# A recommender forward pass on one NeuronCore: one gram matmul a sample, grams and layer 4 moved inside other layers, and one store of rows

## The chip, the cores and the metric

The kernel runs on one core of a Trainium2 chip. The metric is the device time of one execution in microseconds, as the median over runs. In the text, TensorE (PE) multiplies matrices from SBUF into PSUM, VectorE (DVE) and ScalarE (ACT) work elementwise on SBUF and PSUM, GpSimd (POOL) here issues the gathers, and SyncE (SP) issues loads and stores. Each engine runs its own instructions in order; semaphores tie them together.

## What is computed

For each of 512 samples, 26 rows of 128 numbers are fetched from an embedding table, a small dense network adds a 27th, all pairs of the 27 are multiplied, and four dense layers and a last product follow.

```python
fm = emb_table[jnp.arange(N_CAT)[None, :], cat_idx]          # 512 x 26 x 128
h = jax.nn.relu(dense_x @ Wd1 + bd1)                         # 13 -> 512
h = jax.nn.relu(h @ Wd2 + bd2)                               # 512 -> 256
dense = jax.nn.relu(h @ Wdf + bdf)                           # 256 -> 128
Z = jnp.concatenate([fm, dense[:, None, :]], axis=1)         # 512 x 27 x 128
S = jnp.einsum('bie,bje->bij', Z, Z)                         # the gram of a sample, 27 x 27
iu, ju = np.triu_indices(N_CAT + 1, k=1)
x = jnp.concatenate([S[:, iu, ju], dense], axis=-1)          # 351 pairs and dense
x = jax.nn.relu(x @ Wt1 + bt1)                               # layer 1, 479 -> 1024
x = jax.nn.relu(x @ Wt2 + bt2)                               # layer 2, 1024 -> 1024
x = jax.nn.relu(x @ Wt3 + bt3)                               # layer 3, 1024 -> 512
x = jax.nn.relu(x @ Wt4 + bt4)                               # layer 4, 512 -> 256
return jax.nn.sigmoid(x @ Wo + bo)
```

All of it is float32. Layers 2 and 3 split weights and activations into a high and a low float32r part and add three products, (high, high), (low weights), (low activations), in place of one float32 product.

## The kernel before

The batch is cut into four tiles of 128 samples (t = 0 to 3). A start computes the dense network for all samples, and its share of layer 1 (pre), while weights are loaded, split by ScalarE (split_hi) and VectorE (split_lo), and the first rows are gathered. GpSimd issues 104 gathers, one for each tile and feature, into a ring of 38 row buffers (rows); from the 39th on each waits until TensorE has turned the group of features whose buffer it takes.

For every tile, the features come in seven groups g of up to four. TensorE turns a group (transpose_features, L343) into a bank of PSUM (gp), and ScalarE (even g) or VectorE (odd g) copies it into zt (features, L507 and L637), where four samples q stand side by side. Then come the grams (gram, L356): 32 matmuls a tile, each with four samples as 128 stationary columns and the same four as 4 x 27 moving columns. Of each result only the four 27 x 27 blocks on the diagonal are wanted. ScalarE and VectorE copy these out in four rounds (extract, L519 and L645) into s_ij, VectorE turns them in 32 x 32 squares (turn_sums, L653) into xb, both copy the 351 pairs into xp (L524, L655), TensorE turns them in three pieces (transpose_pairs, L369), and ScalarE copies the result to xt (L526). Layer 1 (L380) needs xt.

Layer 1 has 8 column blocks m of 3 matmuls; layer 2 (L409) 48 products in two halves; layer 3 (L429) 24 products n. A sum is added to its bias by VectorE (L659, L670, L681), turned by TensorE (turn, L389) and passed through a relu by ScalarE (L530, L534, L538); VectorE makes the low part (L664, L675). Layer 4 (L445) and the last product (last_layers, L686 and L688) follow, then a sigmoid (L542) and a store of 128 single numbers a tile (L275).

The order on each engine is written out by hand. FEATURES_1, FEATURES_2 and FEATURES_3 say ahead of which m or n of each layer the next tile's feature groups are turned. GRAM_FROM says from which product n of layer 3 on one gram of the next tile follows each product; the rest of the grams stand behind layer 3, with the turn of layer 3's sum after TURN_AFTER of them, then layer 4 and the pairs. Turn 1 of layer 2 (the second half) stands ahead of product 12 of layer 3, which is the first product that needs it:

```python
                    if n == PRODUCTS_3 // 2:
                        turn(t, 1)
                    k, part = n // 3, n % 3
                    if k % 4 == 0 and part == 0:
                        pe.wait_ge(a2_hi, 2 * t + k // 4 + 1)
```

In tile 0 the last copies of features, features(0, 5) on VectorE and features(0, 6) on ScalarE, stand behind the split of the first two pieces of w3.

## Time and profile before

| | |
|---|---|
| Median of 3 runs | 223.09 us (221.65 to 224.78) |
| Span of the profiled execution | 278.7 us |
| Mean granted TensorE clock in it | 0.852 of full speed |
| TensorE matmuls busy | 189.4 us (68%), 976 records |
| TensorE weight loads busy | 148.4 us (53%), 976 records |
| VectorE busy | 82.0 us (29%), 123 |
| ScalarE busy | 66.0 us (24%), 114 |
| GpSimd busy | 104.4 us (37%), 111 |

The profiled execution is some 56 us longer than the timed ones. Busy times are shares of its span. TensorE's matmul time overlaps its weight loads (PEld), and ends of matmuls are modelled.
### The profile page before, as it was taken

To read this page: it belongs to the slowest core of one execution; us is meant where nothing else is said; L and a number is where in the kernel's file an instruction comes from. 1 tells how busy PE (TensorE), PEld (TensorE's weight loads), DVE (VectorE), ACT (ScalarE), POOL (GpSimd) and SP (SyncE) were. 2 spreads that over 40 slices of the span, in tenths; PEclk is the share of its full clock that TensorE was granted. 3 is DMA by queue.
4 is the path that set the end of the run, shared out by engine and by line. 5 is a ranking of instruction groups with operands and counts; after the bars stand their busy time and mean duration, and the time that the engine had idled before them with its cause. 6 is when DMAs were issued, how large, how long until landed. Compare 5 with 4: busy or idle time off the path is not lost.

```text
span 278.7 us, 2407 instructions
## 1 busy us (share of the span) xinstructions
PE 189.4 (68%) x976; PEld 148.4 (53%) x976; DVE 82.0 (29%) x123; ACT 66.0 (24%) x114; POOL 104.4 (37%) x111
## 2 busy tenths in 40 slices
PE   4998630705000249927998974898899999799960
PEld 2334220705000239816697953768698879698630
DVE  3134144001000245311337421134743325431120
ACT  3457534001000233201034310113422124120010
POOL 4777777777774005774640775000000000000000
PEclk9999955775555558995999999799999999799996
DMA  5978868853333001332330235000000000000000
GB/s 122 318 225 226 234 135 251 305 108 52 55 51 45 0 0 22 51 54 35 45 41 4 36 48 45 5 0 0 2 0 0 2 0 0 2 0 0 0 2 0
DMA packets 8885, 17.58 MB, mean 63 GB/s; under 512 B 3249, under 2 KB 4529, under 8 KB 8746
## 3 DMA queue, kind: packets, MB, share of 16 engines
q0 software_dynamic: 3328, 6.82, 15.9%
q1 hardware_dynamic: 5546, 10.60, 11.6%
q8 instruction: 8, 0.13, 0.3%
q14 instruction: 3, 0.02, 0.0%
HBM read 17.41 MB, written 0.00 MB: 62 GB/s over the span
## 4 chain that ended last, share of the span: by engine, by line
PE 45%; another core or an unknown queue 24%; DVE 12%; issue 6%; ACT 5%; DMA 4%; SPq 0%; DVEq 0%
PE mp L409 12%; PE mp L429 9%; PE gp L356 9%; PE tp L380 6%; DMA w<-in_wt 3%; PE gp L343 3%; PE mp L327 3%; DVE s_ij L645 2%; DVE zt L637 2%; DVE xb L653 2%; PE tp L389 2%; ACT w2h L493 2%; DVE a1l L664 1%; PE tp L369 1%
## 5 line engine op out<-in xcount | busy, mean ns | idle before, releaser
L292 POOL DMA_INDIRECT rows<-in_emb,row_of x104 | 103.5, 995 | 66.9 <-PE gp L343 34.8
L356 PE MATMUL gp<-zt 128*128 128x108 f32 x256 | 38.3, 302 | 43.2 <-DVE s_ij L645 26.4
L356 PEld LDWEIGHTS gp<-zt 128*128 128x128 f32 x256 | 37.5, 218 | 45.3 <-ACT s_ij L519 27.5
L645 DVE COPY s_ij<-gp 27x216 f32<-27x216 f32 x32 | 17.0, 531 | 58.1 <-remote 44.2
L519 ACT COPY s_ij<-gp 27x216 f32<-27x216 f32 x32 | 16.6, 519 | 58.6 <-remote 46.2
L409 PE MATMUL mp<-w2h,a1h 128*128 128x512 f32 x64 | 27.2, 425 | 1.8 <-ACT a1h L530 1.8
L380 PE MATMUL tp<-xt,w 117*128 117x128 f32 x192 | 26.5, 297 | 1.5 <-ACT xt L526 1.2
L409 PE MATMUL mp<-w2h,a1l 128*128 128x512 f32 x64 | 26.6, 415 | 0.0
L409 PE MATMUL mp<-w2l,a1h 128*128 128x512 f32 x64 | 26.5, 415 | 0.0
L380 PEld LDWEIGHTS tp<-xt,w 117*128 117x128 f32 x192 | 25.1, 211 | 2.4 <-ACT xt L526 1.5
L343 PE MATMUL gp<-ident,rows 128*128 128x128 f32 x104 | 18.0, 299 | 7.7 <-DMA rows<-in_emb,row_of 5.7
L343 PEld LDWEIGHTS gp<-ident,rows 128*128 128x128 f32 x104 | 14.0, 154 | 11.9 <-DMA rows<-in_emb,row_of 6.3
L507 ACT COPY zt<-gp 128x512 f32<-128x512 f32 (+1 forms) x16 | 8.6, 535 | 39.8 <-PE gp L343 31.1
L637 DVE COPY zt<-gp 128x512 f32<-128x512 f32 x12 | 12.6, 1050 | 16.1 <-PE gp L343 12.1
L633 DVE TENSOR_TENSOR w2l<-w,w2h 128x1024 fp32r<-128x1024 f32 x8 | 9.8, 1222 | 23.2 <-issue 18.0
L409 PEld LDWEIGHTS mp<-w2h,a1h 128*128 128x128 f32 x64 | 12.9, 201 | 4.6 <-ACT a1h L530 2.2
L429 PE MATMUL mp<-w3h,a2h 128*128 128x512 f32 x32 | 13.4, 418 | 2.7 <-ACT a2h L534 2.1
L534 ACT ACTIVATE a2h<-tp 128x512 fp32r<-128x512 f32 x8 | 4.8, 598 | 41.8 <-PE tp L389 26.5
L409 PEld LDWEIGHTS mp<-w2h,a1l 128*128 128x128 f32 x64 | 12.7, 199 | 3.4 <-issue 0.8
L389 PE MATMUL tp<-ident,raw 128*128 128x128 f32 x44 | 7.2, 289 | 10.8 <-DVE raw L670 10.8
L409 PEld LDWEIGHTS mp<-w2l,a1h 128*128 128x128 f32 x64 | 12.6, 198 | 2.3
L429 PE MATMUL mp<-w3h,a2l 128*128 128x512 f32 x32 | 13.6, 424 | 0.0
(61 smaller groups left out, 177.1 us busy)
## 6 DMA issues: line engine op xcount, KB each, us to landing
w<-in_wt SPq DMA_DIRECT2D x13, 512.0 KB
rows<-in_emb,row_of POOLq DMA_INDIRECT x104
w<-in_wt SPq DMA_DIRECT2D x3, 468.0 KB
bc<-in_rows SPq DMA_DIRECT2D x1, 1024.0 KB
wd_sb<-in_wd SPq DMA_DIRECT2D x1, 512.0 KB
w1d<-in_wt SPq DMA_DIRECT2D x1, 512.0 KB
wdf_sb<-in_wdf SPq DMA_DIRECT2D x1, 128.0 KB
out<-probs SPq DMA_DIRECT2D x4, 0.5 KB
```

What stands on the lines that cost most here:

```text
L292: pool.indirect_dma_start(out=rows[:, n % RING, :], out_offset=None, in_=emb.rearrange("c v e -> (c v) e"), in_offset=bass.IndirectOffsetO ...
L343: last = pe.transpose(gp[:, g % 4, n * P:(n + 1) * P], rows[:, (N_CAT * t + f0 + n) % RING, :], ident[:])
L356: last = pe.matmul(gram_banks(r)[:, k // BANK, n * (k % BANK):n * (k % BANK + 1)], zt[:, g, :, :].rearrange("p q f -> p (q f)"), zt[:, g, ...
L380: last = pe.matmul(tp[:, m // 4, (m % 4) * P:(m % 4 + 1) * P], w1[0:PC, k, m * P:(m + 1) * P], xt[0:PC, k, :], start=(k == 0), stop=(k == ...
L389: last = pe.transpose(tp[:, h % 2, c * P:(c + 1) * P], raw[:, h % 2, c * P:(c + 1) * P], ident[:])
L409: last = pe.matmul(mp[:, h, :], a[:, k, :], w[:, k, cols], start=(k == 0 and part == 0), stop=(k == M1 - 1 and part == 2))
L429: last = pe.matmul(mp[:, 0, :], a[:, k, :], w[:, k, :], start=(n == 0), stop=(n == PRODUCTS_3 - 1))
L507: sc.copy(zt_features(g), transposed(g)).then_inc(zt_act, 1)
L519: last = sc.copy(sums(r, q), blocks(r, q))
L633: ve.tensor_tensor(low, weights, high.bitcast(F32), ALU.subtract).then_inc(w_lo, 1)
L637: ve.tensor_copy(zt_features(g), transposed(g)).then_inc(zt_dve, 1)
L645: last = ve.tensor_copy(sums(r, q), blocks(r, q))
```

## The change

- **Grams.** One matmul a sample: 32 stationary columns (27 and zeros) and 27 moving ones, written to the sample's strip of 32 partitions in banks 0 and 1 of gp. 128 matmuls a tile instead of 32. Features are turned in banks 2 and 3 alone (before, all four), so a group waits for the copy of the one two before it.
- **Out of PSUM.** The copies into s_ij are gone; VectorE turns the squares straight out of gp, reading every 32nd number. ScalarE's part of them is gone with them.
- **Order.** For tiles 2 and 3 all grams stand ahead of product 6 of layer 3 and the pairs ahead of product 21; the turn of layer 3's sum and layer 4 move into the next tile's layer 1 (after m = 1 and m = 4), with VectorE's last_layers at its m = 7. For tile 1 the grams stay behind layer 3, with the turn after 8 groups of 4 samples. The second turn of layer 2 moves from product 12 to product 6 in every tile. In tile 0 the last feature copies stand ahead of the split of w3.
- **End.** The logits of all tiles are kept, turned once by TensorE, put through one sigmoid of 4 x 128, and stored as four rows.
- **Memory.** xb and xp get buffers of their own, and the scratch for the gathers' descriptors is 8192 bytes a partition; before, no size was given, and the default is twice that.

```diff
-FEATURES_2 = [{10: [3], 32: [4]}, {4: [3], 26: [4], 46: [5]}, {18: [4], 42: [5]}, {}]
-FEATURES_3 = [{4: [5], 16: [6]}, {10: [6]}, {2: [6]}, {}]
-GRAM_FROM = [PRODUCTS_3, 18, 9, PRODUCTS_3]
+FEATURES_2 = [{10: [3], 32: [4]}, {4: [3], 20: [4], 40: [5]}, {18: [4], 40: [5]}, {}]
+FEATURES_3 = [{2: [5], 16: [6]}, {2: [6]}, {0: [6]}, {}]
+GRAMS_AT = [PRODUCTS_3, 6, 6, PRODUCTS_3]
+PAIRS_AT = PRODUCTS_3 - 3
-TURN_AFTER = 6
+GROUPS_BEFORE_TURN = 8
+TURN_3_AT, LAYER_4_AT = 1, 4
+TURN_2B = 6
...
+        def grams_by_column(n):
+
+            return gp[:, 0:2, :].rearrange("p k (g j) -> p j (k g)", j=SQ)[:, 0:n, :]
...
-            return gp[:, g % 4, 0:nf * P].rearrange(order, f=nf, q=Q)
+            return gp[:, 2 + g % 2, 0:nf * P].rearrange(order, f=nf, q=Q)
...
-            for t in range(TILES):
-                sp.wait_ge(probs_ready, t + 1)
-                sp.dma_start(out[t * P:(t + 1) * P, :], probs[:, t:t + 1]).then_inc(out_done, 16)
-            sp.wait_ge(out_done, 16 * TILES)
+            sp.wait_ge(probs_ready, 1)
+            sp.dma_start(out.rearrange("(t p) c -> t (p c)", p=P), probs[:]).then_inc(out_done, 16)
+            sp.wait_ge(out_done, 16)
...
-                n = Q * NZ
-                last = pe.matmul(gram_banks(r)[:, k // BANK, n * (k % BANK):n * (k % BANK + 1)],
-                                 zt[:, g, :, :].rearrange("p q f -> p (q f)"), zt[:, g, :, 0:NZ], start=True, stop=True)
-                if k == ROUND - 1:
+                for g in range(g0, g1):
+                    for q in range(Q):
+                        c = SQ * (g % 16)
+                        last = pe.matmul(gp[SQ * q:SQ * (q + 1), g // 16, c:c + NZ], zt[:, g, q, :], zt[:, g, q, 0:NZ], start=True, stop=True)
+                if g1 == GROUPS:
                     last.then_inc(gram_ready, 1)
...
+                    if t >= 2 and m == TURN_3_AT:
+                        turn(t - 1, 2)
+                    if t >= 2 and m == LAYER_4_AT:
+                        layer_4(t - 1)
...
-                    if n == PRODUCTS_3 // 2:
+                    if n == GRAMS_AT[t]:
+                        grams(t + 1, 0, GROUPS)
+                    if n == PAIRS_AT and GRAMS_AT[t] < PRODUCTS_3:
+                        transpose_pairs(t + 1)
+                    if n == TURN_2B:
                         turn(t, 1)
...
             layer_4(t)
+            pe.wait_ge(logits_ready, TILES)
+            pe.transpose(mp[:, 0, 0:P], logits[:], ident[:]).then_inc(logits_turned, 1)
...
             def turn_sums(t):
 
-                ve.wait_ge(ex_act, ROUNDS * (t + 1))
-                ve.wait_ge(ex_dve, ROUNDS * (t + 1))
+                ve.wait_ge(gram_ready, t + 1)
                 for x, n in ((xb[:, 0:NZ, :], NZ), (xb[:, NZ:NZ + HALF, :], HALF)):
-                    ve.transpose(x.rearrange("p j i -> p (j i)"), s_ij[:, 0:n, :].rearrange("p j g -> p (j g)")).then_inc(xb_ready, 1)
+                    ve.transpose(x, grams_by_column(n)).then_inc(xb_ready, 1)
...
             split_lo(7)
+            features(0, 5)
             split_lo(M1)
             split_lo(M1 + 1)
-            features(0, 5)
-            for r in range(ROUNDS):
-                extract(0, r)
             turn_sums(0)
...
-    nc = bacc.Bacc("TRN2", target_bir_lowering=False, num_devices=1)
+    nc = bacc.Bacc("TRN2", target_bir_lowering=False, num_devices=1, dynamic_dma_scratch_size=8192)
```

TensorE's order from the end of layer 3 of tile 2 to layer 2 of tile 3. Before, product by product with a gram (gp<-zt) behind each, then the turn of the sum (tp<-ident,raw), the rest, layer 4 (mp<-w,a), the pairs (tp<-ident,xp) and layer 1 (tp<-xt,w):

```order
L429 MATMUL mp<-w3h,a2h 128x512
L356 MATMUL gp<-zt 128x108
L429 MATMUL mp<-w3l,a2h 128x512
L356 MATMUL gp<-zt 128x108
L429 MATMUL mp<-w3h,a2l 128x512
L356 MATMUL gp<-zt 128x108 x7
L389 MATMUL tp<-ident,raw 128x128 x4
L356 MATMUL gp<-zt 128x108 x11
L445 MATMUL mp<-w,a 128x256 x4
L369 MATMUL tp<-ident,xp 117x128 x3
L380 MATMUL tp<-xt,w 128x128 x24
```

The same place now, from product 5 of layer 3 on (the part left out is nine more products):

```order
L424 MATMUL mp<-w3h,a2l 128x512
L344 MATMUL gp<-zt 32x27 x128
L381 MATMUL tp<-ident,raw 128x128 x4
...
L424 MATMUL mp<-w3h,a2l 128x512
L357 MATMUL gp<-ident,xp 117x128 x3
L424 MATMUL mp<-w3h,a2h 128x512
L424 MATMUL mp<-w3l,a2h 128x512
L424 MATMUL mp<-w3h,a2l 128x512
L368 MATMUL tp<-xt,w 128x128 x6
L381 MATMUL gp<-ident,raw 128x128 x4
L368 MATMUL tp<-xt,w 128x128 x9
L436 MATMUL mp<-w,a 128x256 x4
```

All 128 small gram matmuls stand in one block inside layer 3, the pairs three products ahead of its end, and the turn of the sum and layer 4 stand between column blocks of the next layer 1.

VectorE in tile 0, before, from the last split of w2 to the pairs:

```order
L633 TENSOR_TENSOR w2l<-w,w2h 128x1024
L633 TENSOR_TENSOR w3l<-w,w3h 128x1024 x2
L637 COPY zt<-gp 128x4x4x32
L645 COPY s_ij<-gp 27x8x27 x8
L653 STREAM_TRANSPOSE xb<-s_ij 128x864
L653 STREAM_TRANSPOSE xb<-s_ij 128x416
L655 COPY xp<-xb 128x169
```

And now:

```order
L612 TENSOR_TENSOR w2l<-w,w2h 128x1024
L616 COPY zt<-gp 128x4x4x32
L612 TENSOR_TENSOR w3l<-w,w3h 128x1024 x2
L622 STREAM_TRANSPOSE xb<-gp 128x864
L622 STREAM_TRANSPOSE xb<-gp 128x416
L624 COPY xp<-xb 128x169
```

The last feature copy moved ahead of the w3 splits, and the eight copies into s_ij are gone.

TensorE's last rows, before:

```order
L429 MATMUL mp<-w3l,a2h 128x512
L429 MATMUL mp<-w3h,a2l 128x512
L484 MATMUL tp<-ident,raw 128x128 x2
L484 MATMUL gp<-ident,raw 128x128 x2
L445 MATMUL mp<-w,a 128x256 x4
```

And now:

```order
L424 MATMUL mp<-w3h,a2l 128x512
L473 MATMUL tp<-ident,raw 128x128 x2
L473 MATMUL gp<-ident,raw 128x128 x2
L436 MATMUL mp<-w,a 128x256 x4
L477 MATMUL mp<-ident,logits 128x128
```

One turn of the logits is added behind layer 4.

## Rows read from the trace of the kernel before

**Rows 1.** Busy time by stretch: first grams, then tiles 0 to 3.
```profile
core 0: us, PE busy (x) PEld busy (x) DVE busy (x) ACT busy (x) POOL busy (x), PEclk, DMA share, GB/s
49.30:99.40 50.10, 12.84 (x64) 12.20 (x64) 3.14 (x7) 3.08 (x7) 29.31 (x31) 0.57 0.38 85
104.08:154.03 49.95, 41.34 (x238) 35.28 (x238) 18.66 (x28) 12.16 (x23) 25.19 (x26) 0.90 0.25 35
154.03:202.06 48.03, 39.23 (x233) 32.67 (x233) 16.35 (x26) 10.57 (x22) 13.92 (x14) 0.96 0.17 20
202.06:240.44 38.38, 35.92 (x229) 31.47 (x229) 16.40 (x26) 10.82 (x21) 0.00 (x0) 1.00 0.01 0
240.44:270.96 30.52, 27.92 (x140) 22.96 (x140) 7.15 (x13) 3.64 (x8) 0.00 (x0) 0.94 0.01 1
```

**Rows 2.** The page's chain that ended last, share of the span by engine.
```profile
PE 45%; another core or an unknown queue 24%; DVE 12%; issue 6%; ACT 5%; DMA 4%; SPq 0%; DVEq 0%
```

**Rows 3.** Timeline of tile 0's grams: start us, us, what, [idle before].
```profile
49.29 5.40 PE L356 MATMUL gp<-zt 128*128 128x108 f32 x32 [5.28 <-issue]
...
64.32 1.05 DVE L645 COPY s_ij<-gp 27x216 f32<-27x216 f32 x2 [15.17 <-remote]
...
94.44 2.15 DVE L645 COPY s_ij<-gp 27x216 f32<-27x216 f32 x4 [29.07 <-remote]
```

**Rows 4.** The page's groups: busy us, mean ns of one, idle before.
```profile
L356 PE MATMUL gp<-zt 128*128 128x108 f32 x256 | 38.3, 302 | 43.2 <-DVE s_ij L645 26.4
```

**Rows 5.** Timeline from tile 3's last grams to its layer 1.
```profile
233.37 2.54 PEld L356 LDWEIGHTS gp<-zt 128*128 128x128 f32 x22
...
235.92 1.91 PE L445 MATMUL mp<-w,a 128*128 128x256 f32 x8
...
236.12 1.07 DVE L645 COPY s_ij<-gp 27x216 f32<-27x216 f32 x2 [0.72 <-PE gp L356]
237.30 1.57 DVE L653 STREAM_TRANSPOSE xb<-s_ij 128x864 f32<-128x864 f32 x2
...
238.97 0.90 PE L369 MATMUL tp<-ident,xp 128*117 128x128 f32 x3 [1.14 <-ACT xp L524]
...
240.44 6.77 PE L380 MATMUL tp<-xt,w 117*128 117x128 f32 x44 [0.57 <-ACT xt L526]
```

**Rows 6.** Timeline, a round of grams at the lower clock.
```profile
95.61 3.48 PEld L356 LDWEIGHTS gp<-zt 128*128 128x128 f32 x16 [26.63 <-ACT s_ij L519]
```

**Rows 7.** Timeline ahead of tile 0's grams.
```profile
43.32 0.69 PE L343 MATMUL gp<-ident,rows 128*128 128x128 f32 x2 [2.91 <-DMA rows<-in_emb,row_of]
...
46.87 0.38 ACT L507 COPY zt<-gp 128x256 f32<-128x256 f32 x1
...
48.14 1.00 DVE L637 COPY zt<-gp 128x512 f32<-128x512 f32 x1
```

**Rows 8.** Groups with shapes kept apart, a strided copy on VectorE.
```profile
L637 DVE COPY zt<-gp 128x512 f32<-128x512 f32 x12 | 12.6, 1050 | 16.1 <-PE gp L343 12.1 <-remote 4.1
```

**Rows 9.** The chain in order of time (start us, us), products of layer 2.
```profile
209.00 4.13 PE mp L409 x18
```

**Rows 10.** Timeline around the second turn of layer 2, tile 0.
```profile
138.40 0.69 DVE L675 SCALAR_TENSOR_TENSOR a2l<-tp,a2h 128x512 fp32r<-128x512 f32 x1 [1.85 <-issue]
...
138.42 0.51 PE L429 MATMUL mp<-w3h,a2h 128*128 128x512 f32 x1 [0.69 <-issue]
```

**Rows 11.** Waits of SyncE's queue (us, times, longest); a load's landing.
```profile
SPq L79 <- DMA out<-probs: 7.0, 1, 7.0
...
idx<-in_cat_idx SPq DMA_DIRECT2D x1, 52.0 KB, 2.1
```

**Rows 12.** Timeline of GpSimd's 65th gather.
```profile
106.83 1.27 POOL L292 DMA_INDIRECT rows<-in_emb,row_of  x1 [19.02 <-PE gp L343]
```

**Rows 13.** Timeline, two loads of the last turn, and their group.
```profile
266.80 0.20 PEld L484 LDWEIGHTS tp<-ident,raw 128*128 128x128 f32 x2 [0.94 <-DVE raw L748]
...
L484 PEld LDWEIGHTS tp<-ident,raw 128*128 128x128 f32 x2 | 0.2, 141 | 0.9 <-DVE raw L748 0.9
```

174 lines of the change are left out of this document (70 added, 104 removed).

## The prediction

> **What bounds the kernel now.** I read the windows first, tile by tile, because the page averages over stages with different limits. In the stretch of tile 2 (202.06 to 240.44 us, from its first layer 1 matmul to tile 3's) TensorE is busy 35.92 of 38.38 us at full clock, while VectorE has 16.40, ScalarE 10.82 and the gathers nothing [rows 1]. So once it runs, the kernel is bound by TensorE's own instruction stream, plus about 2.5 us a tile in which it waits for somebody.
>
> The profiled execution is not like the timed ones. Its span is 278.7 us and the median of the timed runs 223.09. The chain of waits gives 24% of the span (67 us) to "another core or an unknown queue" [rows 2]. In the timeline TensorE has issued the first two gram rounds by 54.7 us, but VectorE starts copying them only at 64.32, after 15.17 us of such idle time, and the next ones at 94.44, after another 29.07 [rows 3]. Without them the 64 load and matmul pairs begun at 49.3 would have ended near 58 instead of 99.4 (41 us), and tiles 0 and 1 (49.95 and 48.03 us) would be nearer tile 2's 38.38 (11.6 and 9.6 us) [rows 1]. 278.7 less 62 is 216.5, so some 6.5 us of the median lie around the span. I take the stalls to be of the profiled execution alone, make the sum as differences on stretches free of them, and put it on 223.1.
>
> **The change, part by part.**
>
> *The grams.* Before, one matmul makes four samples' gram with 128 stationary and 108 moving columns; the profile counts 256 records for 128 matmuls, so an fp32 matmul is two load and matmul pairs, 64 pairs a tile [rows 4]. Warm, 22 pairs' loads take 2.54 us; less about 0.2 for the last one that is 112 ns a pair, so 7.2 us a tile [rows 5]. Cold, 16 take 3.48 us, less 0.3 for the last one 211 ns a pair [rows 6]. Whether the load's 128 columns or the product's 108 set it does not matter here: both fall to a quarter. After, each sample has a matmul of its own, 32 stationary and 27 moving columns: 128 matmuls, 256 pairs a tile. The trace has no pair this small. Bounds from its rows: if only columns count, 112 x 32/128 = 28 ns; if nothing is saved by being small, 112 ns. The cold and warm figures split a pair into about 99 ns that scales with clock and 13 that does not, which gives 25 + 13 = 38 ns. I take 34, between the two that the load's length supports: 256 x 34 = 8.7 us a tile, 1.5 more than now. Three tiles: +4.6. Tile 0's begin with a cold clock: now 16 pairs cold (3.4 us) and 48 warm (5.4), 8.8; then some 55 pairs in 3.4 us and 201 in 6.8, 10.2: +1.4. Together **+6.0**; every ns on the pair is worth nearly 1 us.
>
> *The start.* VectorE's last feature copy of tile 0 stood behind the split of the w3 weights, which waits for their load; it ran at 48.14 and the grams at 49.29, although TensorE had turned the features by 44.0 [rows 3, 7]. Now both last copies stand ahead of the split: 44.0, plus 0.4 for ScalarE's half-size copy and a handover, is 44.6. **-4.7.** The features now have two banks instead of four, but the copies that free them are done before the last gathers land.
>
> *Between grams and layer 1.* Now it is two copies out of PSUM (1.07), two turns (1.57), a pair copy, TensorE's turn, ScalarE's copy: 236.1 to 240.44, 4.3 us from the last gram on, with layer 4 (1.9 us) inside [rows 5]. The copies go, but VectorE now turns straight out of PSUM with a stride of 32 elements. Not shown by the trace: read as fast as now it stays 1.57 for both turns, 1280 elements; VectorE's strided copies cost 2.05 ns an element (512 in 1050 ns) [rows 8], which would make it 2.6. At tile 0 and on the way to tile 1 the whole chain stays exposed: between -1.1 and 0 each, I take **-1.0** for both. On the way to tiles 2 and 3 the grams stand after 6 of 24 products of layer 3, and 15 products of 0.23 us (3.4) [rows 9] and a turn (0.4) cover the chain. VectorE must first do the low part of layer 2, done at 139.09, 2.0 us after the turn begins (138.42 less 0.69 of idle time and 0.6 of turning) [rows 10], then 2.0 to 3.1 us of turns and copy: ready 4.0 to 5.1 us after the last gram against cover of 3.8. The waits that go are 1.7 us plus a stretched turn, 2.2; what comes is 0.3 to 1.5 us. **-2.6** for two. Layer 4 and its turn move into the next layer 1 at the same price; the sum it turns should be ready 0.8 us after layer 3 and is asked for after 12 pairs of layer 1 (1.3). If that cover fails, 1 us a tile returns. VectorE's last layers stand there between the two sums of layer 1; layer 2 needs the second only after 12 products (2.8 us), so that wait hides.
>
> *The second turn of layer 2* moves from product 12 to 6, away from the product that waits for its ScalarE copy: 0.69 us of idle time each tile goes [rows 10], **-2.8**.
>
> *The clock.* Tile 3's stretch has a granted clock of 0.94, tile 2's 1.00 [rows 1]: after the idle gap the first matmuls of layer 1 run at the lower of the two levels. With no gap, 0.06 x 30.5 us, **-1.8**.
>
> *The store.* At the end SyncE waits 7.0 us for the last of four stores of 128 four-byte pieces [rows 11]. Now one store of four rows of 512 bytes. A load of 52 KB lands in 2.1 us [rows 11]; I take 2.6 for it: -4.4, between 0 (if a store's reply costs 7 whatever its form) and -4.9. A turn of the logits and its handovers are added, +0.5; the three other sigmoids and stores were hidden. **-3.9.**
>
> *The scratch* is halved for the gathers. They are paced by GpSimd: the 31 of the first window run to 87.8 us and the next waits 19 us for TensorE [rows 1, 12]. At 1.25 us each, tile 1's last is issued at 72, and the new kernel asks for it near 78; the later tiles' are earlier still. Nothing, unless less room makes GpSimd wait.
>
> Sum: 6.0 - 4.7 - 1.0 - 2.6 - 2.8 - 1.8 - 3.9 = -10.8, 223.1 to **212 us**. Everything but the grams is -16.8; the change breaks even at 45 ns a pair.
>
> A rule speaks against it. The Trainium skill, page "TensorE: Matmul & The Clock Gate", section "Wait — 56ns, not 53.3ns?", says that matmul starts never come closer than about 25 ns, and that where instructions are decoded in software each MATMUL costs about 62 ns, which binds when the array's work is shorter. By the first my 34 stands; by the second, as an estimate, grams take 15.9 us a tile and the sum gives about 240. No pair in this trace is short enough to tell.
>
> **The rivals.**
>
> *A. The price is per instruction, not per column* (slower). The two loads of the last turn, with a matmul between them, take 0.20 us together and 0.14 each, so they begin 0.06 us apart, after a wait in which they could queue up; I found none closer [rows 13]. If that is what a pair costs in a long stream, 15.4 us a tile: 3 x 8.2 + 6.6 = 31, less 16.8, 237 us; at the upper bound of 112 ns, 28.7 us a tile, about 290. For it: four times the instructions for the same arithmetic, and the trace's distances have a part that does not scale. Against it: that part is 13 ns. It decides from 45 ns; from 50 the kernel is over 2% slower. 0.25. The page above names the same price.
>
> *B. Four samples run side by side.* The four matmuls of a group write to four different strips of 32 partitions of PSUM. If their loads and products overlap, a pair may cost 15 to 25 ns: 3.8 to 6.4 us a tile, 192 to 203 us. Nothing in the trace speaks for or against it. The Trainium skill, page "TensorEngine Tiling (Array Packing)", section "Theoretical Speedup", gives up to 4 times for a dimension of 32. 0.10.
>
> *C. The gains do not arrive.* The chain out of PSUM is at its dear end, the store still waits 7 us, the start finds another load late, or narrow matmuls do not hold the clock, so that layer 3's rest runs at the lower level (about 1.7 us a tile): 218 to 227 us. 0.15.
>
> **How the numbers follow.** The forecast has 0.50: 28 ns and the cheap ends give 203, 38 ns and the dear ends 219. About 2% is what a measurement of this kernel tells from no change, 218.6 to 227.6. Faster: 0.50 less a tail, and B: 0.60. Same: C and the edges of the forecast and A: 0.15. Slower: 0.25. For 8 in 10 I go from 199 (leaving out most of B) to 239 (A at 60 ns inside, the higher prices out). The forecast's own range is 203 to 219.
>
> **What the changed profile would show.** Groups of 256 gram loads 28 to 38 ns apart and 8 to 10 us long; the copies into s_ij gone; turns out of PSUM of 1.1 to 1.9 us (864 elements); layer 1 of tiles 2 and 3 less than 1.5 us behind layer 3; no lower clock at tile 3; the first gram at 44 to 45 us; the last store's wait under 3 us. A gram stage over 11.5 us would make the prediction wrong by itself. A long stream that again shows unexplained waits for TensorE's results in the profile alone would not.

## The result and the profile after

The changed kernel takes 198.81 us (median of 4 runs, 196.33 to 200.24), the kernel before beside it 222.49: ratio 0.884, 95% interval 0.875 to 0.893. A second measurement, further down, gave 0.891 (0.882 to 0.900). I take the middle of the two, 0.8875, for the changed kernel; 1% of the kernel before is 2.2 us. It is faster, as forecast, but by about 25 us and not by 11: below the range, which began at 199. Ratios leave disturbed runs out, so they can differ from the ratio of the medians.

The stretches of the changed kernel: the start up to the first gram; tile 0's grams up to layer 1; then from one tile's layer 1 to the next one's, and to the end (columns as in [rows 1]).

```profile
core 0: us, PE busy (x) PEld busy (x) DVE busy (x) ACT busy (x) POOL busy (x), PEclk, DMA share, GB/s
0.00:46.30 46.30, 30.61 (x70) 12.76 (x70) 14.12 (x17) 21.43 (x31) 33.82 (x38) 0.89 0.80 231
46.30:58.80 12.50, 5.17 (x259) 4.50 (x259) 4.38 (x5) 2.95 (x5) 9.76 (x10) 0.50 0.67 195
58.80:97.40 38.60, 36.43 (x429) 31.40 (x430) 14.54 (x20) 8.28 (x14) 29.34 (x31) 0.90 0.39 54
97.40:129.40 32.00, 29.99 (x415) 25.62 (x414) 10.72 (x15) 5.83 (x11) 24.20 (x26) 0.99 0.38 54
129.40:163.50 34.10, 30.98 (x424) 26.50 (x422) 11.79 (x18) 6.53 (x12) 7.90 (x9) 1.00 0.14 20
163.50:195.70 32.20, 28.55 (x154) 23.52 (x153) 8.70 (x17) 4.13 (x8) 0.00 (x0) 1.00 0.00 1
```

The span is 195.7 us and that execution's time 197.5, so only 1.8 us lie around the span, not the 6.5 that I had assumed.

I had the kernel before profiled once more, unchanged, since its first profile held 67 us of unexplained waits [rows 2]:

> The kernel before, unchanged, for a second profile. Theory 1 (the waits for TensorE's results belonged to that one profiled execution): its span comes out near 220 us, close to the timed 222.5, with no idle time of 10 us or more put down to an unknown release. Theory 2 (they are the kernel's own): the same 15 and 29 us gaps stand in tile 0's grams again and the span is near 279 us.

It took 222.75 us, and none of those waits was there. They belonged to one execution, as assumed. Its stretches serve from here on as those of before:

```profile
0.00:47.50 47.50, 30.78 (x71) 12.99 (x71) 17.28 (x19) 23.41 (x32) 34.71 (x38) 0.89 0.78 222
47.50:62.70 15.20, 11.67 (x68) 11.06 (x68) 6.24 (x11) 5.30 (x11) 11.49 (x13) 0.72 0.65 187
62.70:104.50 41.80, 39.80 (x237) 34.46 (x237) 18.68 (x28) 12.26 (x23) 32.04 (x33) 0.94 0.36 52
104.50:145.80 41.30, 38.52 (x234) 33.44 (x234) 16.30 (x26) 10.62 (x22) 26.57 (x29) 0.96 0.33 48
145.80:185.90 40.10, 37.64 (x230) 33.14 (x230) 16.39 (x26) 10.79 (x21) 0.00 (x0) 0.96 0.01 0
185.90:223.90 38.00, 27.93 (x140) 22.98 (x140) 7.15 (x13) 3.65 (x8) 0.00 (x0) 0.88 0.01 1
```

This profiled execution took 225.7 us, 3 more than the median of the timed ones, so its differences are a little large: start -1.2, tile 0's grams to layer 1 -2.7, then -3.2, -9.3, -6.0, -5.8; 28.2 us in all. Part of that is the clock of this one execution: it had a granted clock of 0.910 over the whole, the other execution of the same kernel 0.944. The kernel before_one_store further down, which does the same up to the end, has 13.5, 41.2, 39.8 and 38.5 us for the stretches from tile 0's grams to tile 3's layer 1, with clocks of 0.87, 0.96, 1.00 and 1.00. Against those the differences are -1.0, -2.6, -7.8 and -4.4. From tile 2 on the two kernels move work between stretches: layer 4 and a turn (2.2 us) leave the stretch of tile 1 for that of tile 2, and those of tile 2 for tile 3's.

Now the gram block of tile 3, in the stretch of tile 2, as the timeline has it (start us, us, what, [idle before]):

```profile
153.49 1.56 PEld L344 LDWEIGHTS gp<-zt 128*32 128x32 f32 x174 [0.37 <-issue]
153.50 1.67 PE L344 MATMUL gp<-zt 128*32 128x27 f32 x174
157.58 0.80 PEld L344 LDWEIGHTS gp<-zt 128*32 128x32 f32 x82 [2.52 <-issue]
157.59 0.90 PE L344 MATMUL gp<-zt 128*32 128x27 f32 x82 [2.42 <-issue]
158.42 0.66 PE L381 MATMUL tp<-ident,raw 128*128 128x128 f32 x4
```

The last row of loads has 82 pairs in 0.80 us; less about 0.1 for the last load that is 8.6 ns a pair. I had forecast 34, and bounded it from below by 28. Then there is something that [rows 5] and [rows 6] do not have: after 174 pairs TensorE stands still for 2.42 us, waiting for nothing that the profile shows ("issue"). Tile 0's grams show the same, at the lower clock:

```profile
46.32 2.28 PE L344 MATMUL gp<-zt 128*32 128x27 f32 x149 [0.46 <-ACT zt L498]
53.26 1.74 PE L344 MATMUL gp<-zt 128*32 128x27 f32 x107 [4.67 <-issue]
55.29 1.58 DVE L622 STREAM_TRANSPOSE xb<-gp 128x864 f32<-128x864 f32 x2 [5.69 <-PE gp L344]
57.02 1.16 PE L357 MATMUL gp<-ident,xp 128*117 128x128 f32 x3 [2.02 <-ACT xp L507]
```

At the full clock a block of 256 pairs is thus 2.2 us of pairs; the other 2.6 to 3.9 us of tiles 1 to 3 are waits (in tile 1 with the turn that stands in its block). From its first load to its last it takes 6.05, 5.3 and 4.8 us on the way to tiles 1, 2 and 3, where the 64 pairs of before stand for 7.2, and 8.4 in tile 0, where before_again has 10.1 (before_one_store, whose clock rose earlier, 8.7). Where the profile says "issue", the queues tell more. The changed kernel's page has this row, and before_again's has 8 packets in it:

```profile
q8 instruction: 14, 0.23, 0.5%
```

0.23 MB in 14 packets is 16 KB a packet. The changed kernel has 6 packets more and, with 1745 pairs of a load and a matmul recorded instead of 976, 1538 such instructions more; by estimate a packet is 256 of them, and a block of 256 pairs is two packets. DMA activity between 153 and 160 us consists of two such packets, at 155.0 and 158.7 us.

### The profile page after: what moved, and what is told of

Same layout as the page of the kernel before. It is cut to its first block, busy times and chain, and to the rows that moved or that the text cites. A ratio compares the mean times of both kernels' runs of the same rounds, so it can differ in the third digit from the quotient of the medians.

```text
span 195.7 us, 3866 instructions
## 1 busy us (share of the span) xinstructions
PE 161.7 (83%) x1745; PEld 124.3 (64%) x1745; DVE 64.3 (33%) x91; ACT 49.1 (25%) x79; POOL 105.0 (54%) x111
## 4 chain that ended last, share of the span: by engine, by line
PE 67%; POOL 14%; issue 10%; DMA 4%; DVE 2%; ACT 1%; DVEq 0%
PE mp L401 23%; POOL rows L281 14%; PE tp L368 12%; PE mp L424 11%; PE gp L344 7%; PE gp L333 5%; PE mp L436 4%; DMA rows<-in_emb,row_of 3%; PE tp L381 2%; PE gp L357 1%; DMA idx<-in_cat_idx 1%; DVE xb L622 1%; DVE zt L616 1%; PE gp L381 0%; DVE z L655 0%
## 5 line engine op out<-in xcount | busy, mean ns | idle before, releaser
L401 PE MATMUL mp<-w2h,a1h 128*128 128x512 f32 x64 | 26.0, 407 | 0.7 <-DVE z L655 0.7
L401 PE MATMUL mp<-w2l,a1h 128*128 128x512 f32 x64 | 25.6, 400 | 0.0
L401 PE MATMUL mp<-w2h,a1l 128*128 128x512 f32 x64 | 25.4, 398 | 0.0
L344 PE MATMUL gp<-zt 128*32 128x27 f32 x1024 | 13.6, 205 | 11.7 <-issue 10.8
L344 PEld LDWEIGHTS gp<-zt 128*32 128x32 f32 x1024 | 11.9, 120 | 14.6 <-issue 13.7
L401 PEld LDWEIGHTS mp<-w2h,a1h 128*128 128x128 f32 x64 | 12.1, 189 | 3.2 <-DVE z L655 0.9
L644 DVE SCALAR_TENSOR_TENSOR a2l<-tp,a2h 128x512 fp32r<-128x512 f32 x8 | 5.5, 692 | 24.4 <-ACT a2h L517 24.4
L424 PE MATMUL mp<-w3h,a2l 128*128 128x512 f32 x32 | 12.8, 400 | 0.0
L424 PE MATMUL mp<-w3l,a2h 128*128 128x512 f32 x32 | 12.7, 397 | 0.0
L639 DVE TENSOR_TENSOR raw<-mp,bc 128x512 f32<-128x512 f32 x8 | 5.5, 692 | 20.8 <-PE mp L401 20.8
```

The source lines that it names most:

```text
L344: last = pe.matmul(gp[SQ * q:SQ * (q + 1), g // 16, c:c + NZ], zt[:, g, q, :], zt[:, g, q, 0:NZ], start=True, stop=True)
L401: last = pe.matmul(mp[:, h, :], a[:, k, :], w[:, k, cols], start=(k == 0 and part == 0), stop=(k == M1 - 1 and part == 2))
L424: last = pe.matmul(mp[:, 0, :], a[:, k, :], w[:, k, :], start=(n == 0), stop=(n == PRODUCTS_3 - 1))
L639: ve.tensor_tensor(raw[:, h, :], mp[:, h, :], bc[:, ROW2 + h * HALF2:ROW2 + (h + 1) * HALF2], ALU.add).then_inc(raw_ready, 1)
L644: ve.scalar_tensor_tensor(out=a2l[:, 4 * h:4 * h + 4, :].rearrange("p m b -> p (m b)"), in0=tp[:, h, :], scalar=0.0, in1=a2h[:, 4 * h:4 * ...
```

## Experiments

**What a pair of narrow matmuls costs.** Three kernels. The first has the changed gram's order of samples turned inside out, so that 32 neighbours write to one strip of 32 partitions of PSUM before the next strip begins:

```diff
-                for g in range(g0, g1):
-                    for q in range(Q):
+                for q in range(Q):
+                    for g in range(g0, g1):
```

> The changed kernel with the gram loops exchanged: 32 matmuls in a row go to the same strip of 32 PSUM partitions before the next strip's. Theory B (the price of 9 to 10 ns comes from four strips at work at once): pairs 25 to 34 ns apart, 6.5 to 8.7 us a gram stage with the instruction waits hidden inside, so 1 to 3 us a tile more, 200 to 209 us. Rival (a narrow pair is that cheap anywhere): pairs stay at 10 ns and the time at 197 to 199.

It took 204.21 us, ratio 0.911 (0.900 to 0.922), 5 us more than the changed kernel. Its block for tile 3:

```profile
159.34 7.88 PEld L344 LDWEIGHTS gp<-zt 128*32 128x32 f32 x256 [0.37 <-issue]
```

7.88 us less 0.1 over 255 steps is 30.5 ns a pair, and there is no wait. So the same instructions with the same operands cost about 3.6 times as much when neighbours share a strip. The second kernel lets neighbours alternate between two strips:

```diff
-                for g in range(g0, g1):
-                    for q in range(Q):
+                for h in range(2):
+                  for g in range(g0, g1):
+                    for q in (2 * h, 2 * h + 1):
```

> The changed kernel with a block's gram matmuls in two passes: first samples q = 0 and 1 of all groups in turn, then q = 2 and 3, so that neighbours alternate between two strips of 32 partitions and not four. Measured so far: with neighbours in one strip a pair's load starts 31 to 32 ns after the last, with four strips about 8.5 ns. Theory 1 (matmuls in different strips run side by side, each strip taking 31 to 32 ns a pair): two strips give 15.5 to 16 ns, 256 pairs in 4.1 us. Theory 2 (the supply of instructions holds the average at 256 pairs in 4.5 to 5 us at either rate): waits of 0.5 us or longer stay but add up to less than 1 us, the stage ends up as long as with four strips, and the time is the same as the changed kernel's within 2%, 197 to 201 us. If the rate alone decided, the stage would be 4.1 - 2.2 = 1.9 us a tile longer and the kernel 5 us or more slower, 204 or more. Rival to both: only the step from one strip to another matters, so two strips already give 8.5 ns.

```profile
118.81 3.52 PEld L345 LDWEIGHTS gp<-zt 128*32 128x32 f32 x219 [0.36 <-issue]
153.94 2.77 PEld L345 LDWEIGHTS gp<-zt 128*32 128x32 f32 x174 [0.37 <-issue]
158.31 1.40 PEld L345 LDWEIGHTS gp<-zt 128*32 128x32 f32 x82 [1.60 <-issue]
```

2.77 us less 0.1 over 173 is 15.4 ns, half of 30.5. One, two and four strips give 30.5, 15.4 and 8.5 ns: strips run side by side. Yet the kernel took 197.36 us, ratio 0.883 (0.876 to 0.891), the same as with four. A pair costs nearly twice as much and the end has not moved: the wait ahead of the last loads is 1.60 instead of 2.52. The four blocks together last 26.6 us instead of 24.5, which is no more than these ratios can tell. That was theory 2 of its expectation: for the most part something else paces the block.

The third kernel is the kernel before with nothing but the small matmuls:

```diff
-                last = pe.matmul(gram_banks(r)[:, k // BANK, n * (k % BANK):n * (k % BANK + 1)],
-                                 zt[:, g, :, :].rearrange("p q f -> p (q f)"), zt[:, g, :, 0:NZ], start=True, stop=True)
+                for q in range(Q):
+                    c = n * (k % BANK) + NZ * q
+                    last = pe.matmul(gram_banks(r)[32 * q:32 * (q + 1), k // BANK, c:c + NZ], zt[:, g, q, :], zt[:, g, q, 0:NZ], start=True, stop=True)
```

> The kernel before with one change: each sample has its own gram matmul (32 stationary, 27 moving columns), written to the place where the old copies expect it; all else stays. Theory of the forecast (a small pair costs 34 ns): about 6 us slower than before, 228. Theory B (four strips overlap, a pair costs about 10 ns as in the profile of the changed kernel, with waits of 2 to 5 us a tile in the stream): gram stages of 3 to 6 us instead of 7, 3 to 8 us faster than before, 214 to 219; the part that the copies of each round still hold back is not gained.

It took 220.54 us, ratio 0.986 (0.978 to 0.994): 3 us faster, where pairs at 8.5 ns would save 5 us a tile. Three things eat the gain. One is the copies in four rounds that the grams still wait for. The second is the clock, below. The third shows where grams stand between products of layer 3:

```profile
168.15 0.26 PE L358 MATMUL gp<-zt 128*32 128x27 f32 x8
168.34 0.51 PE L430 MATMUL mp<-w3h,a2h 128*128 128x512 f32 x1
168.78 0.27 PE L358 MATMUL gp<-zt 128*32 128x27 f32 x8
```

From one group of 8 pairs to the next is 0.63 us. A product is 0.23 [rows 9] and 8 pairs are 0.07, so 0.33 us is lost on every round trip between narrow and full-width matmuls. Before, two full-width pairs and a product took 0.46 in the same place (173.42 to 173.88 in before_again), which is 0.23 + 0.22 and loses nothing. As for the clock: in the profile its stretch from tile 0's grams to layer 1 has 0.50, where before_again has 0.72, and the mean of its executions is lower too (0.89 to 0.91, against 0.92 to 0.94 for the executions of before that the ratios use).

**The waits.** If TensorE runs ahead of its instructions, other work between the narrow pairs should hide the waits. First in small portions:

```diff
-                    if n == GRAMS_AT[t]:
-                        grams(t + 1, 0, GROUPS)
+                    if GRAMS_AT[t] < PRODUCTS_3 and n >= SPREAD_FROM and GROUPS > SPREAD * (n - SPREAD_FROM):
+                        grams(t + 1, SPREAD * (n - SPREAD_FROM), min(GROUPS, SPREAD * (n - SPREAD_FROM + 1)))
```

with SPREAD_FROM, SPREAD = 4, 3.

> The changed kernel with the grams of tiles 2 and 3 given out in threes of four samples ahead of products 4 to 14 of layer 3 instead of in one block ahead of product 6. Theory F (the waits of 1.9 to 2.6 us inside each gram block are TensorE waiting for its next instructions, which a stream of pairs 9 ns apart uses up faster than they are fetched): with 0.23 us products between them the waits go, 3 to 5 us in both tiles together, 193 to 196 us. Rival (the waits are a limit on the number of matmuls or loads in flight and come with the count): they reappear between the products and the time stays at 197 to 199.

197.37 us, ratio 0.882 (0.870 to 0.893): no change. The long waits are gone in tiles 2 and 3, and the switches have taken their place:

```profile
156.51 0.39 PE L345 MATMUL gp<-zt 128*32 128x27 f32 x24
156.84 0.50 PE L425 MATMUL mp<-w3l,a2h 128*128 128x512 f32 x1
157.27 0.39 PE L345 MATMUL gp<-zt 128*32 128x27 f32 x24
```

0.76 us a round, of which 0.23 is the product and 0.20 the pairs: 0.33 again, 11 times a tile. Then in three blocks, with the dictionary {4: (0, 11), 8: (11, 22), 12: (22, 32)} of products and groups:

> The changed kernel, but for tiles 2 and 3 the 256 gram pairs stand in three blocks of 88, 88 and 80 ahead of products 4, 8 and 12 of layer 3, in place of one block ahead of product 6. In the changed kernel's profile these two stages last 5.41 and 4.92 us, of which about 2.2 are pairs 8.5 ns apart and the rest waits of 1.7 to 2.4 us that coincide with 16 KB instruction packets on queue 8. Theory 1 (the waits are TensorE running ahead of its instruction supply; four products of 0.23 us between blocks let the supply catch up): the long waits go, three changes between narrow and full-width matmuls of about 0.3 us each come in place of one, so each stage costs about 2.2 + 0.9 = 3.1 us over the products, 1.8 to 2.3 us less; with two tiles 3 to 4.5 us less, about 195 us. Theory 2 (the waits come with a fixed number of fetches wherever the narrow pairs stand, and lie on the path all the same): no change, 198 to 200 us. Theory 3 (each change of width costs more than 0.3 us, or the later pairs hold up layer 1): 1 us or more longer.

195.28 us, ratio 0.875 (0.868 to 0.881). Against 0.8875 that is 2.8 us less. By its profile, the stretches of tiles 1 and 2 are 30.7 and 32.8 us long instead of 32.0 and 34.0, 1.3 and 1.2 us less, which agrees; theory 1 had put it at 1.8 to 2.3, since it left out that the blocks still have short waits inside.

The profile names no releaser for the wait, but the observations leave little beside instructions. Packets of 16 KB on the instruction queue stand beside each wait, and each wait ends a nearly fixed time behind one. The traces of the ten profiled executions with two or four strips, after_spread and after_again among them, and of before_small_grams hold 36 waits of more than 1 us between narrow pairs that nothing else releases. They last 1.1 to 6.5 us, and in all 36 the pairs go on 1.25 to 1.6 us after the end of such a packet. In the changed kernel the packets end at 51.78, 91.71, 122.16 and 156.23 us, and the pairs go on at 53.26, 93.14, 123.53 and 157.58. The wait in tile 0 is the longest because its packet comes late: it begins at 50.7, 2.2 us into the wait.

The rest agrees: in tile 0 the break comes after exactly 149 pairs in the changed kernel, in after_two_strips (149 pairs in 4.02 us, then 2.10 of wait, where the changed kernel has 2.28 and 4.67), in every other kernel here with two or four strips, and in before_small_grams (128 and 21); at 30.5 ns a pair it vanishes (the one gap left, 0.7 us after 64 pairs in tile 1, is the turn that stands there); and work put between shortens it. Where the wait begins is a place in the program, not a time or an operand; where it ends is a packet. What a packet waits for I did not find out.

**The second turn of layer 2.** In the changed kernel TURN_2B = 12 again:

> The changed kernel with the second turn of layer 2 at product 12 of layer 3 again instead of product 6. Forecast for this part: 0.69 us of TensorE's idle time a tile comes back, 2.8 us in all, about 201.5 us. In the profile the product behind the turn should show about 0.7 us of idle time in every tile, as it does in the profile of before. Rival: for tiles 2 and 3 the turns out of PSUM now stand in VectorE's queue ahead of nothing that this turn needs, but the grams at product 6 give ScalarE and VectorE about 5 us, so only some tiles pay: 1.4 us or less, within what a measurement can tell, 198 to 200 us.

206.23 us, ratio 0.926 (0.917 to 0.934): 3.8%, 8.4 us, against a forecast of 2.8. Waits for a2h are as forecast, four of 0.69 us:

```profile
PE mp L424 <- ACT a2h L517: 2.7, 4, 0.7
```

But the turn costs more than its idle time. In before_again it begins at 207.17 and the next product at 208.46, 1.29 us for what takes 0.41 where nothing waits (158.42 to 158.83 in the changed kernel), and the next two products follow after 0.34 and 0.38 us, where they follow after 0.32 and 0.23 without the wait: about 1.05 us a tile, not 0.69. And the clock falls, here in tile 2:

```profile
162.30:164.00 1.70, 1.70 (x19) 1.39 (x8) 0.00 (x0) 0.00 (x0) 0.00 (x0) 0.70 0.04 10
164.00:166.00 2.00, 1.64 (x6) 0.94 (x5) 0.00 (x0) 0.32 (x1) 0.00 (x0) 0.50 0.00 0
```

0.50 is the lower level, 1.2 GHz. The stretches of tiles 1 and 2 have a granted clock of 0.95 here, 0.99 and 1.00 in the changed kernel. Each of the two falls, at 125.4 and 163.0, lasts 3.4 us, which is 1.7 us of work. Four turns at 1.05 and two falls at 1.7 are 7.6 us, and the profiled executions differ by 7.7 (203.4 against 195.7). The falls begin 2.4 and 1.6 us ahead of the turn, behind the gram block with its wait, so the gap at the turn does not start them, and the changed kernel has such blocks without a fall; I can say what a fall costs, but not what starts it. To see whether the price exists without the small grams, the same edit alone in the kernel before (TURN_2B = 6 instead of PRODUCTS_3 // 2):

> The kernel before with one edit, the second turn of layer 2 at product 6 of layer 3 in place of 12. Forecast for this part: 0.69 us of idle time a tile, 2.8 us in all, ratio 0.987. Rival 1: undoing this edit in the changed kernel cost 7.4 us (206.2 to 198.8), so it may be worth as much here, ratio 0.967; the product behind the turn starts 1.28 us after the turn in the profile of before, where four transposes need 0.41, and part of its tile then runs at the lower clock. Rival 2: the cost in the changed kernel came of the waits of the small grams meeting the turn, which the kernel before doesn't have: 2.8 to 4 us.

217.22 us, ratio 0.978 (0.964 to 0.992): 4.9 us, with 1.8 to 8.0 in the interval. So the edit is worth about 5 us by itself, near the 4.2 of four turns at 1.05, and about 8 once the grams stand ahead of the turn.

**The store.** The changed kernel with four sigmoids and four stores of single numbers again, without the turn of the logits:

```diff
-            sp.wait_ge(probs_ready, 1)
-            sp.dma_start(out.rearrange("(t p) c -> t (p c)", p=P), probs[:]).then_inc(out_done, 16)
+            for t in range(TILES):
+                sp.wait_ge(probs_ready, t + 1)
+                sp.dma_start(out[t * P:(t + 1) * P, :], probs[:, t:t + 1]).then_inc(out_done, 16)
```

> The changed kernel with a sigmoid and a store of 128 single numbers a tile again, without the turn of the logits. Forecast for this part: the last store's wait 7.0 us in place of 2.6, less 0.5 for the turn of the logits that is left out, 3.9 us. The changed kernel's profile shows a wait of 0.9 us for the one store of rows, so if the reply to single numbers takes 7.0 us again, the difference is 7.0 - 0.9 - 0.5 = 5.6 us, about 204 us. If the wait depends on the session and not on the form (the unchanged kernel's store also landing in 1 to 3 us), the difference is 0 to 2 us, 198 to 200 us.

202.89 us, ratio 0.918 (0.913 to 0.922), 3.0% or 6.7 us. The other way round, the one store in the kernel before:

> The kernel before with the end of the changed one: logits of all tiles kept, turned once, one sigmoid, one store of four rows; and the smaller scratch for the gathers, without which the logits find no room in SBUF (that edit by itself measured 0.9943, 0.9873 to 1.0013). Forecast for this part 3.9 us, ratio 0.983; from the profiles 6.7 us of waiting against 0.9, less about 1.2 for the turn of the logits and its handovers, 4.6 to 5.3 us, ratio 0.977; undoing it in the changed kernel cost 4.1 us by the medians and up to 7.5 us by the ratios. If the store's reply depends on anything but its form, 0 to 2 us.

216.18 us, ratio 0.979 (0.969 to 0.989), 4.6 us. SyncE's last wait in the changed kernel (us, times, longest), and in after_four_stores:

```profile
SPq L78 <- DMA out<-probs: 0.9, 1, 0.9
```

```profile
SPq L78 <- DMA out<-probs: 6.6, 1, 6.6
```

It is 6.7 in before_again and 0.9 in before_one_store. The form of the store decides, 5.8 us (before_one_store also has the smaller scratch, which by itself changes nothing, see below). Against it stand the turn and its handovers, of which the wait for z (0.99 us) is the largest part. The last stretch of the profiles, from tile 3's layer 1 to the end, puts the whole between the two ratios: 37.5 against 32.2 us with and without four stores in the changed kernel, 38.0 against 32.8 in the kernel before.

**The start.** The last two feature copies of tile 0 behind the split of w3 again:

> The changed kernel with the last two feature copies of tile 0 behind the split of w3 again, as before the change. My forecast for this part was 4.7 us: first gram at 49.3 instead of 44.6. If the forecast holds, this kernel takes 4 to 5 us longer than the changed one, about 203 us, and its first gram stands near 49 to 51 us. Rival: the profiles show the first gram at 46.3 in the changed kernel (the last gathers land at 45.1, and TensorE turns them at 45.2) and at 47.5 in the unchanged one run again, so the load of w3 and its split vary from execution to execution and are worth only 1 to 2 us: about 200 us.

199.89 us, ratio 0.901 (0.895 to 0.907): 1.3% or 3 us, between the two expectations. Its profile shows why the forecast could not be met:

```profile
44.30 1.23 DVE L612 TENSOR_TENSOR w3l<-w,w3h 128x1024 fp32r<-128x1024 f32 x1 [0.33 <-ACT w3h L484]
45.44 1.00 DVE L616 COPY zt<-gp 128x512 f32<-128x512 f32 x1
46.59 2.06 PE L344 MATMUL gp<-zt 128*32 128x27 f32 x132 [2.06 <-DVE zt L616]
```

The copy does stand behind the split, and TensorE waits 2.06 us for it. But without that the first gram is no earlier than the rows: in the changed kernel the turn of the last features waits for the gathers until 45.16, and the first gram stands at 46.32. Both move by a microsecond or two from one execution to the next.

**The order.** All grams, the turn of layer 3's sum, layer 4 and the pairs behind layer 3 in every tile:

```diff
-GRAMS_AT = [PRODUCTS_3, 6, 6, PRODUCTS_3]
+GRAMS_AT = [PRODUCTS_3] * 4
```

with the statements of t == 0 used for every tile.

> The changed kernel, but the grams, the turn of layer 3's sum, layer 4 and the pairs stand behind layer 3 for every tile, as they do for tile 1, instead of inside layer 3 and inside the next layer 1 for tiles 2 and 3. Theory (the exposed chain is worth what the forecast said): in the changed kernel 3.5 us pass on the way to tile 0 from the first turn out of PSUM to layer 1, of which layer 4 (1.7 us) and a turn (0.4) can lie inside on the way to tiles 2 and 3, so 1.3 to 2.5 us a tile are exposed: 3 to 5 us for two tiles, 201 to 204 us. Rival (now that a tile's grams take little time, the place of grams and layer 4 does not matter, and the change in order has only moved waits): within 1 us of the changed kernel. A third case: TensorE's clock falls in the wait and layer 1 starts at the lower of the two levels, which adds 1 to 2 us a tile: 205 us or more.

197.85 us, ratio 0.886 (0.881 to 0.891): the rival holds, no difference. The way to tile 3 there:

```profile
162.96 1.12 PE L344 MATMUL gp<-zt 128*32 128x27 f32 x108 [1.52 <-issue]
164.01 2.00 PE L432 MATMUL mp<-w,a 128*128 128x256 f32 x8
165.85 0.86 PE L357 MATMUL gp<-ident,xp 128*117 128x128 f32 x3
167.28 0.49 PE L368 MATMUL tp<-xt,w 117*128 117x128 f32 x2 [0.57 <-ACT xt L504]
```

With VectorE turning straight out of PSUM, layer 4 (1.84 us) covers the turns, and the pairs follow without a gap. From the pairs' end (0.43 us after 165.85) to layer 1 is all that stands idle, 1.0 us. That is what the move inside layer 3 can save a tile, and in the changed kernel much of it is spent again: in tile 2, though not in tile 3, the first product of layer 2 waits 0.70 us for VectorE's z, and a gram block takes longer there (5.3 and 4.8 us, against 4.6 and 4.8 here with a turn of 0.4 inside).

**The scratch.** Only dynamic_dma_scratch_size=8192 in the kernel before:

> The kernel before with one edit, 8192 bytes a partition of scratch for the gathers' descriptors instead of the default. Forecast: nothing, 220 to 224 us, within the interval of before; GpSimd issues a gather every 1.25 us at either size. Rival: half the room makes GpSimd wait for descriptors to be used up, seen as longer waits between gathers; up to 20 us later with the last gather, but still ahead of the tiles that need it, so the time changes only if tile 1's gathers come after 80 us.

224.00 us, ratio 0.994 (0.987 to 1.001), no difference; a gather's median is 944 ns against 947 in before_again. Its use, which no run shows, is meant to be the room that it leaves in SBUF for the wider logits.

**All of it together.** Three blocks for tiles 1, 2 and 3, tile 0's layer 4 inside tile 1's layer 1, and TensorE's wait for z moved to the second half of layer 2, whose bank it guards:

```diff
-                at_least(pe, z4_ready, t)
+                    if h == 1 and k == 0 and part == 0:
+                        at_least(pe, z4_ready, t)
...
-GRAMS_AT = [PRODUCTS_3, 6, 6, PRODUCTS_3]
+GRAMS_AT = [6, 6, 6, PRODUCTS_3]
-FEATURES_3 = [{2: [5], 16: [6]}, {2: [6]}, {0: [6]}, {}]
+FEATURES_3 = [{0: [5], 2: [6]}, {2: [6]}, {0: [6]}, {}]
```

> The changed kernel with three edits: the grams of tiles 2 and 3 in three blocks ahead of products 4, 8 and 12 of layer 3; the same for tile 1 (with its last two feature groups at products 0 and 2, and the turn of layer 3's sum and layer 4 of tile 0 inside layer 1 of tile 1); and TensorE's wait for VectorE's z moved from the first product of layer 2 to the first of its second half. Expected from the changed kernel's profile: on the way to tile 1 the two long waits (1.95 and about 0.7 us) and the exposed chain from the last gram to layer 1 (4.1 us less 1.75 of layer 4) go, and the half clock in that stretch with it: 3 to 5 us; the three blocks on the way to tiles 2 and 3 bring 1.2 us each by the profile of that kernel, 2.5 us; the wait of 0.7 us for z goes: 0.7 us. Sum 6 to 8 us: 191 to 193 us. If the switches of width and VectorE's queue take it back: 195 us, as with the three blocks alone. If the clock falls for want of work ahead of layer 1, it would be seen as half clock at the start of layer 1 of tiles 1 to 3.

191.93 us, ratio 0.863 (0.857 to 0.869), 5.4 us faster than the changed kernel and the fastest kernel here. Its stretches of tiles 0 to 3:

```profile
58.30:93.20 34.90, 32.09 (x416) 27.19 (x417) 12.97 (x17) 7.75 (x13) 26.67 (x28) 0.96 0.36 53
93.20:125.10 31.90, 31.84 (x427) 26.95 (x426) 12.23 (x19) 6.42 (x12) 24.28 (x26) 1.00 0.37 55
125.10:157.40 32.30, 31.65 (x424) 26.40 (x422) 11.93 (x18) 6.54 (x12) 12.87 (x14) 1.00 0.23 31
157.40:189.60 32.20, 28.54 (x154) 23.55 (x153) 8.70 (x17) 4.13 (x8) 0.00 (x0) 1.00 0.00 1
```

3.7 us come on the way to tile 1, where the exposed chain and the lower clock (0.90 to 0.96) go. The stretch of tile 1 is as long as in the changed kernel (31.9 against 32.0) although it has taken in 2.2 us of layer 4 and a turn. TensorE is now busy 31.84 of 31.90 us in it.

**The changed kernel again**, to narrow what all of these are compared with:

> The changed kernel unchanged, to narrow what the others are compared with: 196 to 200 us, ratio 0.884. If the ratio comes out above 0.893, the parts undone so far cost less than their ratios say by that much; below 0.875, more.

196.80 us, ratio 0.891 (0.882 to 0.900); within what was expected.

## Why the prediction was wrong, step by step

- **The grams: the step that failed.** "28 ns if only columns count" was taken as the lower bound of a pair. It is one only for neighbours in the same strip; there the forecast of 34 stands against 30.5 measured (7.9 us a tile, forecast 8.7). Matmuls to four strips overlap, 8.5 ns, and the supply of instructions brings the block back to 4.8 to 6.05 us. The forecast for the term was +6.0. The four blocks are now 8.4 + 6.05 + 5.3 + 4.8 = 24.5 us, the old ones 8.7 to 10.1 and 3 x 7.2, so 30.3 to 31.7: -6 to -7. That step alone is 12 to 13 us of TensorE's time. Not all of it reaches the end: from one strip to four the blocks lose 9.6 us (34.1 to 24.5), the kernel 5 by the ratios and 8.8 between the two profiled executions. In tile 0 the wait of 4.67 us goes with the clock: the stretch from the first gram to layer 1 has 0.50, with one strip 0.75. Over whole executions, the span times the share of the clock that was not granted is 14 to 18 us in the changed kernel and 8.5 with one strip, in the executions that the ratios use.
- **Rival B was this mechanism**, with a chance of 0.10 and 15 to 25 ns; the effective price (4.8 to 6.05 us over 256 pairs) is 19 to 24. I had no row for or against it, put it at 0.10 and cut it off from the range. It deserved more: the destinations in the diff are four different strips, and of a mechanism that no row speaks of either way 0.10 was a guess on one side. The Trainium skill, page "TensorEngine Tiling (Array Packing)", section "Key Properties", says that tiles operate independently and can do loads and matmuls in parallel; the runs agree, with 30.5, 15.4 and 8.5 ns. It also says there that changing the mode drains TensorE; the 0.33 us of a round trip would fit that, but no run here shows that a drain is its cause.
- **Rival A fell.** No pair costs 60 ns. The rule of the Trainium skill, page "TensorE: Matmul & The Clock Gate", section "Wait — 56ns, not 53.3ns?", of at least about 25 ns between starts and about 62 ns where decoding in software binds, is not what these rows show with four strips: 82 loads and 82 matmuls in 0.80 us. With one strip, 30.5 ns, the first part is not contradicted.
- **The second turn of layer 2** had the right mechanism, and its size was off: 0.69 of idle time is 1.05 with the overlap that is lost on both sides of it, which makes 4.2 and not 2.8 for four tiles, and two falls of the clock came on top where the grams stand ahead of the turn. 4.9 us alone, 8.4 undone, forecast 2.8.
- **The store** too: 2.6 us of wait assumed by a load's landing [rows 11], 0.9 measured; 4.6 to 6.7 for the whole by the ratios, 5.2 to 5.3 by the profiles, forecast 3.9.
- **The clock** at -1.8 was looked for only at tile 3, and as a sum it did not come. The changed kernel's tiles 1 to 3 have 0.99, 1.00 and 1.00, but before_one_store has 1.00 in tiles 1 and 2 as well (before_again 0.96 in both), and what the later tiles gain, tile 0 gives back: 0.50 up to layer 1 against 0.72 and 0.87. Span times the clock not granted is 12 to 19 us, 16.2 on average, in the 30 executions of the kernel before that the ratios of the experiments use, and 14 to 18, 15.6 on average, in the 8 of the changed one.
- **The start** was too large: 4.7 forecast, about 3 by the ratios, 1.2 between the profiles. The first gram at 44.6 came from rows of one execution in which the gathers were done by 43.3 [rows 7]; they land at 45.1 here.
- **The chain for tiles 0 and 1** (-1.0) came out: from the last gram to layer 1 it is 4.1 and 4.2 us, against 4.7 and 4.6 in before_one_store.
- **The chain for tiles 2 and 3** (-2.6) and the order: nothing measured. I counted the wait that goes (2.2) and not that layer 4 had covered most of the chain already, once the copies into s_ij are gone. The chain did shorten, from 4.7 us (181.2 to 185.88 in before_again) to 3.4 with the old order (163.9 to 167.28 above), which the missing copies explain; no run takes the copies out alone. The 0.70 us that layer 2 waits for z in tile 2 I had not listed: I had looked at the second sum of layer 1 and called that wait hidden, but z, which stands behind a feature copy there, is what the first product asks for.
- **The turn out of PSUM** costs what it did from SBUF; the bound of 2.05 ns an element [rows 8] never came into it:

```profile
L653 DVE STREAM_TRANSPOSE xb<-s_ij 128x864 f32<-128x864 f32 x4 | 4.3, 1078 | 0.4
```

```profile
L622 DVE STREAM_TRANSPOSE xb<-gp 128x864 f32<-128x864 f32 x4 | 4.3, 1078 | 11.2 <-PE gp L344 11.2
```

- **The scratch** at nothing was right, and so was leaving the 67 us of unknown waits out.

Without the overlap, after_one_strip is what I had priced: 0.911, 202 us beside 221.5. So 5 us of the error come of the overlap as it reaches the end. Narrow pairs that are cheaper even in one strip bring 2 to 3.5 (blocks of 34.1 us, so +2.4 to +3.8 and not +6.0), the turn 2 to 6 and the store 1 to 3; the start and the chain brought about 4 less than forecast. With the middle of each that is some 10 us of 14. The rest is open; each of these ratios can tell about 2 us. These prices hold the clock's part already, so it is not counted again.

## What to carry to other kernels

When many small matmuls replace few large ones, ask first where each one writes: neighbours in different strips of 32 partitions overlap, those in one strip do not, and that is a factor of about 3.6. Once they are that cheap, what bounds them is the instruction stream and the change of width; here blocks of some 80 pairs with several large products between did best. A gap of 0.7 us ahead of a product cost 1.05, since the turn ahead of it and the products behind it lost their overlap too. And look at the clock of a whole execution, not only at the stretch that was changed: the waits between cheap pairs in tile 0 went with the lower clock. Four bytes a row is a dear form for the last store.

## What the runs showed of the hardware

- Narrow fp32 pairs (32 stationary, 27 moving columns) start 30.5 ns apart in one strip, 15.4 in two, 8.5 in four. A full-width pair takes 112 ns [rows 5].
- A round trip from full width to narrow and back costs 0.33 us, with 8 pairs or 24 between.
- TensorE can run ahead of its instructions: in the changed kernel's blocks it stood still after 239, 219 and 174 pairs for 1.8 to 2.5 us, and after 149 in tile 0 for 4.7 (3.3 to 6.4 over the kernels with four strips), where the weight loads hold the DMA engines (share 0.70 from 50 to 53 us). It went on 1.25 to 1.6 us after a packet of 16 KB on the instruction queue had ended, 36 times of 36. That the packet brings the instructions is inferred from this.
- VectorE's 32 x 32 turn reads PSUM at a stride of 32 elements as fast as packed SBUF: 1078 ns for 864.
- The last wait of SyncE for a store of 128 single numbers was 6.6 to 7.0 us, for one of four rows of 512 bytes 0.9.
